# A fused convolution and gating kernel: in its last stage ScalarE issues the stores in its own DMA queue, SyncE only the loads

## The reference

```python
x = x + conv3x3_depthwise(sign(group_norm(x)), sign(kernel))         # layer 0
v = group_norm(x)
xc = v * ca_gate                                                      # a gate per image and channel
x2 = xc * sigmoid(y) + xc * sigmoid(s)                                # y, s: one value per pixel
out = x + relu((x2 - mean(x2)) * rsqrt(var(x2) + EPS) * bn_gamma + bn_beta)
```

## Time and profile before

| | |
|---|---|
| median of 3 runs | 3281.34 us (3279.26 to 3291.13) |
| the profiled execution, its time | 3285.82 us |
| its span, first to last instruction | 3284.0 us |
| busy: PE / PEld / DVE / ACT | 77% / 50% / 90% / 82% of the span |
| DMA queue of SP (hardware_dynamic) | 1223.41 MB, 92.4% of the 16 engines' span |
| mean granted TensorE clock | 0.851 |

### The profile page before, as it was taken

How to read it: one execution, slowest core, us unless ns; L and a number is a source line. 1 busy time by engine, 2 the same in 40 slices (tenths; PEclk the granted TensorE clock), 3 DMA queues, 4 the chain that set the end, 5 groups by cost and what they waited for, 6 DMA issues and landing times. The chain is left out here.

```text
span 3284.0 us, 50167 instructions
## 1 busy us (share of the span) xinstructions
PE 2531.5 (77%) x17105; PEld 1633.0 (50%) x17105; DVE 2971.8 (90%) x4057; ACT 2701.3 (82%) x3772; POOL 57.1 (2%) x111
## 2 busy tenths in 40 slices
PE   7899999999999999999987333333566766667776
PEld 5566666666666666666442000000455555555555
DVE  8789998999988999889986899999999999999997
ACT  6788888888888888888774688888799888888887
POOL 3000000000000000000001200000000000000000
PEclk9999999999999999999998555555688878787777
DMA  8899999999999999999866699999599999999998
GB/s 315 321 374 409 376 369 371 373 409 382 368 365 372 406 383 371 367 365 395 280 171 169 264 421 421 420 421 418 236 429 428 429 429 428 429 429 429 429 429 363
DMA packets 199097, 1228.49 MB, mean 374 GB/s; under 512 B 29792, under 2 KB 38936, under 8 KB 157644
## 3 DMA queue, kind: packets, MB, share of 16 engines
q1 hardware_dynamic: 195884, 1223.41, 92.4%
q0 software_dynamic: 2976, 2.00, 0.3%
HBM read 805.14 MB, written 420.17 MB: 373 GB/s over the span
## 5 line engine op out<-in xcount | busy, mean ns | idle before, releaser
L1449 PE MATMUL psum<-signs,taps 128*128 128x448 f16 x4032 | 856.5, 355 | 40.7 <-DVE signs L1078 31.8
L1568 PE MATMUL psum<-signs,picked 12*128 12x448 bf16 x896 | 314.5, 491 | 340.7 <-DMA signs<-gate_scratch 271.0
L1449 PEld LDWEIGHTS psum<-signs,taps 128*128 128x128 f16 x4032 | 385.2, 98 | 367.2 <-DVE signs L1078 51.3
L2001 DVE SCALAR_TENSOR_TENSOR xc<-xt,curs,psum 128x1792 f32<-128x1792 f32 x222 | 452.1, 2078 | 57.0 <-PE psum L1568 45.5
L841 ACT ACTIVATE xt<-psum 128x896 f32<-128x896 f32 x416 | 377.9, 910 | 143.6 <-PE psum L1347 129.7
L1781 DVE SCALAR_TENSOR_TENSOR xc<-xt,curs,psum 128x1792 f32<-128x1792 f32 x224 | 455.8, 2079 | 33.3 <-PE psum L1568 32.3
L1710 ACT ACTIVATE xc<-xc 128x1792 f32<-128x1792 f32 x224 | 380.1, 1697 | 95.2 <-DVE xc L1781 95.2
L1129 DVE CUSTOM_DVE_ANT_0 xt<-work,xt 128x896 f32<-128x896 int8 x416 | 436.0, 1086 | 13.7 <-ACT work L849 13.6
L1347 PE MATMUL psum<-ident,stage 128*128 128x128 f32 x3066 | 410.6, 276 | 22.0 <-DMA stage<-x_dram 12.3
L1972 ACT ACTIVATE xc<-xc,bn,curs 128x1792 f32<-128x1792 f32 x224 | 411.7, 1903 | 13.8 <-DVE xc L2001 4.7
L857 ACT ACTIVATE work<-xt,mean 128x1792 bf16<-128x1792 f32 x208 | 370.2, 1780 | 29.2 <-DVE x1max_p L1129 29.2
(11 more groups left out here) (221 smaller groups left out, 2953.2 us busy)
## 6 DMA issues: line engine op xcount, KB each, us to landing
xt<-x_scratch SPq DMA_DIRECT2D x210, 1792.0 KB, 25.3
stage<-x_dram SPq DMA_DIRECT2D x219, 896.0 KB, 10.0
xc<-x_scratch SPq DMA_DIRECT2D x210, 896.0 KB, 9.3
x_scratch<-xt SPq DMA_DIRECT2D x208, 896.0 KB, 9.3
out_dram<-stage SPq DMA_DIRECT2D x75, 1792.0 KB, 21.9
out_dram<-work SPq DMA_DIRECT2D x37, 1792.0 KB, 21.9
x_scratch<-last_unit SPq DMA_DIRECT2D x16, 896.0 KB, 10.2
signs<-ssm_scratch SPq DMA_DIRECT2D x14, 448.0 KB, 4.7
```

Of the source, the lines that this page charges most:

```text
L1449: return nc.tensor.matmul(turn[h % 2][:, b * 512:b * 512 + HB], taps[:, j, t, :], signs[:, j, r:r + RT // 2, dw:dw + W], start=t == 0, sto ...
L1568: last = nc.tensor.matmul(dst[:, b, :], picked[:, b * P:(b + 1) * P], gate_rows[:, s * BW:(s + 1) * BW], start=True, stop=True)
L2001: nc.vector.scalar_tensor_tensor(quarters(xc[m % 2][:, j, :]), slot_quarters(s, j), curs[:, h, j:j + 1], gate_quarters(gate_ps4), ALU.add, ...
```

## The change

SP loses the wait for `staged` and the store. ACT gets both: the store of strip m - 1 stands behind the ReLU of strip m + 1 and ahead of the wait for a free output buffer and the copies of strip m. The last strip of each written-out or looped piece is stored at the end of that piece, ahead of the next ReLU. `image_of` gives the image, from a register in the loop. The transfers themselves, their sizes and buffers are the same.

```diff
@@ sync
                     while fetched < TOTAL and fetched - NS + behind(fetched) <= m:
                         fetch(fetched)
                         fetched += 1
-                    sp.wait_ge(staged, (m + 1) * TG + E4)
-                    sp.dma_start(out_strips[(m // NS - 2) % NB, m % NS * SP:(m % NS + 1) * SP, :].rearrange("(p t) c -> p t c", t=NT),
-                                 outs[m % NO][:, :, :]).then_inc(written[m % NO], 16)
                 for b in range(NO):
                     sp.wait_ge(written[b], 16 * turns(b, NO, TOTAL) + W4)
@@ scalar
+                def image_of(it, m):
+                    if isinstance(it, int):
+                        return (m // NS - 2) % NB
+                    return it * (BODY // NS) + (m // NS - 2)
+
+                def store(it, m):
+                    act.wait_ge(staged, count(it, m, TG) + TG + E4)
+                    nc.scalar.dma_start(out_strips[image_of(it, m), m % NS * SP:(m % NS + 1) * SP, :].rearrange("(p t) c -> p t c", t=NT),
+                                        outs[m % NO][:, :, :]).then_inc(written[m % NO], 16)
+
                 relu(0, 0)

                 def step(it, m0, n):
                     for m in range(m0, m0 + n):
                         if m + 1 < TOTAL:
                             relu(it, m + 1)
+                        if m > m0:
+                            store(it, m - 1)
                         act.wait_ge(written[m % NO], count(it, m, 16, NO) + W4)
                         for k in range(TG):
                             act.wait_ge(turned4, count(it, m, TG) + k + 1 + T4)
                             nc.scalar.activation(outs[m % NO][:, 2 * k:2 * k + 2, :].rearrange("p t c -> p (t c)"),
                                                  out_ps[k % 4], ACT.Identity).then_inc(staged, 1)
+                    store(it, m0 + n - 1)
```

## The result

The changed kernel takes 3296.38 us (median of 5 runs, 3290.21 to 3297.11) against 3281.34 us before (also 5 runs, 3279.26 to 3291.13). The ratio is 1.0035, 95% interval 1.0024 to 1.0046: slower by 8 to 15 us, clear of noise, and under the 0.5% at which the prediction drew its line. The profiled execution has a span of 3295.3 us, 11.3 us more than before. 3.0 of these lie ahead of the touched stage: its first load is issued at 2333.15 instead of 2330.11 us, after code that is the same (in the other traces of this study that moment lies between 2326 and 2333 us). The stage itself, from its first load to the end, grew from 953.9 to 962.1 us, by 8.2.

What follows compares the result with a forecast made beforehand. The prediction took the last stage to be bound by DMA bytes; 0 + 0 - 2 + 6 - 1 = +3 us gave 3288.8 against the profiled 3285.8, or 3284 beside the median of 3281.3, range 3270 to 3301.

Steps and rivals of the forecast that it cites:

- step 4: End of the last stage: with two queues less work is in flight at the last load, +6 us (0 to +15).
- step 1: Last stage's transfers: same bytes at the same rate with two queues, 0 us; bounds -17 us (437 GB/s) and +19 (420).
- rival B: Last stage: two queues move less, loads and stores alternating by packet; at 420 GB/s 3303 us; chance 0.13.
- ACT's issues, 0 us: Last stage: ACT issues 112 stores, its sequencer running ahead under the ReLU, so no engine time is lost, 0 us.
- Rival C: Last stage: ACT becomes the bound if issuing holds the engine; with 2 us per strip +56 us, 3337; chance 0.05.
- The earlier load, -2 us: Start of the last stage: SP, without the wait for `staged`, issues the second load 2 us earlier, -2 us.
- step 5: Tail of the last stage: with less in flight ACT's last waits for stores go, -1 us.
- Rival D: Last stage: loads overtake stores, which fall behind, with no gain at the start; 3296 us, +0.46%; chance 0.07.

## Why the prediction was right, and where its sum was not

It forecast no change within 0.5% and a time of 3284 in 3270 to 3301. The median came to 3296.4, in the range, and just outside the 3278 to 3296 that the prediction gave for its own mechanism. The sum had the right sign, but was about three times too small or more (+3 forecast, +8 in the stage's trace, 8 to 15 by the ratio). The sign was luck: the plus came from step 4, which the runs don't bear out, and the time was lost in step 1, which had been put at 0. What held was the bound: the DMA is full, the bytes are the same, and the rate stayed within the two rows that step 1 named. Step by step:

1. *Bytes and rate, 0 us.* This term was mis-sized. The rate fell from 429 to 424 GB/s, +8.9 us over 800 us, inside the bounds of -17 and +19 that the step had set. It is a mild rival B. The reason given for 0, that the same mix is the nearest row, left out that packets of both queues alternate (in 72% of the pairs after a large load packet) and that landings change (stores 13.1 us instead of 22.4). What was lost is the time in slow packets, 14.5 us per engine instead of 6.3, and why they are slow is open (below).
2. *ACT's issues, 0 us.* Right. Each takes 0.338 us of the sequencer under the ReLU, and the run with 322 issues by ScalarE in one queue stands at 1.0003. Rival C falls with it.
3. *The earlier load, -2 us.* The load did come 2.1 us earlier. The step forgot the other side of the same strip: the first store came 2.4 us later, behind a ReLU that waited for DVE. The DMA's idle time in the first 30 us shrank by 0.8 us, not 2, and over the whole stage not at all (10.5 us in both).
4. *Work in flight, +6 us.* It assumed equal shares, and the stores at their limit. The shares weren't equal: 11 turns against 9, and the loads stood at their limit, the reverse of what was forecast (11 to 15 us for loads, 22 for stores, where 26 and 13 came). With equal turns (gate rows split, or left out) the stores do stand at their limit, at 22 us, but the loads land in 18 to 20. So what the step overlooked is the weight of small packets. The sum of the term was wrong as well. The last load is issued 912.7 us after the first instead of 901.7, but the tail from there is 49.4 us instead of 52.2: of the 11.0 us, 8.2 are left at the end, which the slower rate covers alone (8.3 us by the unrounded rates). A shorter queue at the last load is a shorter tail, and the -1 of step 5 was 2.8. I had taken the tail as set by DVE and ACT, while the earlier trace rows show it with a DMA share of 0.72 on average only, full at first. That work in flight is worth nothing as long as the DMA is full is argued from this, not shown: the run meant to test it changed the rate too.
5. *Rival D* named loads overtaking stores. The opposite took place.

What stays open is why a few packets take twice as long. The runs narrow it. It isn't ScalarE's issuing (1.0003), nor which kind stands in which queue (swapped, 1.0043), nor, but for a small part, the second queue as such (1.0007 by estimate without the small packets, 1.0002 with half of the loads in it), and it comes with one queue too when loads are held to 18 us (1.0050). Where the scarcer kind had about 1.2 transfers in flight (landing 13 us, less 2.3, over 8.6 us per strip) the ratio was 1.003 to 1.004; where it had 1.8 to 2.3, at most 1.0016, but for the one-queue run just named. That is a pattern, not a cause, and it covers neither the two kernels with stores from both queues, which lost most, nor the one with loads from both, where every second load landed in some 13 us and the times show no loss. Whether the memory has a part in it was not tested.

## What to carry to other kernels

In this stage, whose DMA is full, another queue brought no bandwidth: none of the ten kernels with two queues moved more than 429 GB/s in a window of 200 us. It changed who waits. The two queues shared an engine by packets (90% of the small ones of SyncE's queue were followed by one of ScalarE's), so that a trickle of small packets, 0.3% of the bytes, decided which stream stood at its limit; keep small transfers off the stream that is critical or split them evenly (half of the loss here), and look at landing times on both sides after any such move. And count a stretch at the DMA's ceiling as bound by bytes only together with the rate itself: a share of 1.01 went with 429, 424 and 417 GB/s.

## What was not expected of the hardware

Moving 24 small packets per strip from one queue to the other turned landings of 26 us for loads and 13 for stores into 13 and 22. A DMA share of 1.01 went with 429 and with 417 GB/s, 3% less, since the time in slow packets counts as busy: over the 200 us at 417 GB/s the time above 535 ns was 5.8 us per engine, in the same window of the kernel before 0.7. Stores of neighbouring strips from two queues cost 1.0% to 1.4% of the whole kernel, loads from two queues nothing that the times show (1.0002, 0.9993 to 1.0012).
